# Sharing runs of eight edge records between blocks, and two pieces of work moved inside the edge loops of a two-layer graph kernel

## The reference, cut to what matters

```python
# layer 0: attention over edges, keyed by src
score = a_s[:, src] + a_d[:, dst] + aw_e[:, None] * elem[None, :] + ab[:, None]
w = jnp.exp(-jax.nn.relu(score / 20.0))
pooled = segment_sum(w * feats[:, dst], src); row_sum = segment_sum(w, src)
out = pooled / row_sum
# then a mixture of 16 experts, top 2
# layer 1: relations, keyed by dst
rel_e = rel_emb[etype]
alpha = exp(leaky_relu(h[src] @ w_src + h[dst] @ w_dst + rel_e @ w_rel))[:, None]
alpha = alpha / sum(alpha, axis=1, keepdims=True)      # one column: alpha is 1
agg = segment_sum((h[src] + rel_e) @ weight_neighbor * alpha, dst)
# then a dense feed-forward over the better half of the nodes
```

## Time and profile before

| | |
|---|---|
| time before, median of 3 runs | 2547.16 us (2541.32 to 2551.01) |
| the profiled execution | 2546.9 us, span 2545.2 us |
| busy over the span | PE 70%, DVE 77%, POOL 54%, ACT 14% |
| first stage (sort of layer 0, its table) | to 321 us |
| edge loop of layer 0 | 321 to 938 us |
| expert stage | about 1053 to 1467 us |
| edge loop of layer 1 | about 1585 to 2266 us |

### The profile page before, as it was taken

How to read it: one execution, slowest core, us unless ns; L and a number is a source line. 1 busy time by engine, 2 the same in 40 slices (tenths; PEclk the granted TensorE clock), 3 DMA queues, 4 the chain that set the end, 5 groups by cost and what they waited for, 6 DMA issues and landing times. The chain is left out here.

```text
span 2545.2 us, 41027 instructions
## 1 busy us (share of the span) xinstructions
PE 1787.7 (70%) x9989; PEld 1323.2 (52%) x9989; DVE 1962.6 (77%) x5413; ACT 367.8 (14%) x1302; POOL 1377.7 (54%) x1250
## 2 busy tenths in 40 slices
PE   0699357777777745499999934666666666567997
PEld 0698234445444424489998923333333333335776
DVE  8987898888888866587777356788888888776395
ACT  0000100000000002012221214011111111014331
POOL 0486077777777720148888500777777777610200
PEclk9999766676777655699999967677787786667999
DMA  2000144554545551589998841777767777941001
GB/s 91 2 4 12 52 119 133 133 131 133 132 132 133 126 54 52 184 283 293 295 298 279 277 143 59 214 203 201 198 195 199 196 199 196 155 61 35 27 0 50
DMA packets 204203, 361.38 MB, mean 142 GB/s; under 512 B 37152, under 2 KB 111580, under 8 KB 203996
## 3 DMA queue, kind: packets, MB, share of 16 engines
q0 software_dynamic: 64000, 175.79, 27.5%
q1 hardware_dynamic: 139196, 181.82, 23.1%
q10 hardware_dynamic: 928, 2.75, 0.3%
HBM read 334.42 MB, written 25.84 MB: 142 GB/s over the span
## 5 line engine op out<-in xcount | busy, mean ns | idle before, releaser
L960 POOL DMA_INDIRECT e_rows<-table,e_gidx x952 | 925.1, 972 | 322.5 <-issue 277.7
L1197 PE MATMUL e_psO<-e_rows,e_oh 128*128 128x260 f32 x928 | 382.2, 570 | 34.6 <-DVE acc L1025 29.4
L1025 DVE TENSOR_TENSOR acc<-acc,e_psO 128x260 f32 (+1 forms) x708 | 349.7, 494 | 47.3 <-PE e_psO L1197 12.9
L1925 PE MATMUL e_psO<-e_rows,e_oh 128*128 128x456 bf16 x488 | 232.4, 476 | 149.9 <-DVE e_oh L1887 149.8
L1197 PEld LDWEIGHTS e_psO<-e_rows,e_oh 128*128 128x128 f32 x928 | 233.7, 274 | 123.8 <-DVE acc L1025 68.6
L1098 PE MATMUL e_psA<-e_own_of_unit,e_ohT 128*128 (+2 forms) x952 | 115.0, 179 | 210.1 <-DVE e_sc L1154 111.9
L1098 PEld LDWEIGHTS e_psA<-e_own_of_unit,e_ohT 128*128 128x128 bf16 x952 | 86.3, 99 | 328.6 <-issue 318.8
L640 POOL DMA_INDIRECT records<-ordered,s_chunk x68 | 122.0, 1793 | 119.2 <-ACT ordered L625 103.3
L1927 PE MATMUL e_psO<-e_rows,e_oh 128*128 128x256 bf16 x488 | 172.5, 353 | 0.0
L1926 PE MATMUL e_psO<-e_rows,e_oh 128*128 128x256 bf16 x488 | 171.9, 352 | 0.0
L1491 POOL DMA_INDIRECT ln_xn<-token_rows,slot_row x64 | 99.3, 1552 | 126.2 <-POOLq L102 104.8
(11 more groups left out here) (367 smaller groups left out, 3655.1 us busy)
## 6 DMA issues: line engine op xcount, KB each, us to landing
hot_run<-in_L_ffn_w_dram SPq DMA_DIRECT2D x107, 512.0 KB, 6.2
XN<-in_L_ffn_w_dram SPq DMA_DIRECT2D x85, 512.0 KB, 5.0
e_edge_row<-edge_rows SPq DMA_DIRECT2D x122, 256.0 KB, 4.3
e_rows<-table,e_gidx POOLq DMA_INDIRECT x952, 3.0
e_edge_row<-edge_rows SPq DMA_DIRECT2D x116, 128.0 KB
table<-frow SPq DMA_DIRECT2D x25, 192.5 KB, 2.2
table<-frow SPq DMA_DIRECT2D x25, 130.0 KB, 1.9
token_rows<-ln_xn SPq DMA_DIRECT2D x25, 128.0 KB, 1.7
```

Source lines behind the costliest of these rows:

```text
L960: pool.indirect_dma_start(out=rows[:, r, t, 0:width], out_offset=None, in_=table, in_offset=bass.IndirectOffsetOnAxis(ap=gidx[:, r, t:t + ...
L1025: v.tensor_tensor(d, d, psO[:, units * (r % (4 // units)) + j, 0:accw], ALU.add).then_inc(S["added"], 1)
L1197: return pe.matmul(out[:, 0:A0], oh[:, r, t, :], rows[:, r, t, :], start=start, stop=stop)
L1925: pe.matmul(out[:, 0:A1], lhs, row[:, 2 + 2 * D:T1 + R], start=start, stop=False)
```

## The change

1. **Numbering through all blocks.** `starts` first sums the counts over the blocks of a bucket, so that a bucket's edges are numbered through all 17 blocks without padding between them. Where one block's run ends inside a chunk, the next block goes on in the same chunk. The scatters of both blocks name that chunk, so each scatter now adds (`compute_op=ALU.add`) to a list that was set to zero, and a block's scatters wait until the earlier block's scatters to the same list have landed. Layer 0 has two such lists for alternate blocks (`COPIES = (2, 1)`); both are loaded and one DVE addition (`merge`) joins them.
2. **Fewer units.** The formula loses the padding by blocks: 439 units in place of 463 in layer 0 (110 groups in place of 116), 232 in place of 244 in layer 1 (116 in place of 122). A block may now hold two partial chunks a bucket, so its matrices have 109 rows (ROWS) in place of 104; the scatters still name 112.
3. **Layer 1's marks and running counts in the loop of layer 0.** The 26 compares and 17 scans leave the first stage. DVE's loop in layer 0 does two compares in every four groups for 13 turns, then two scans in every four groups for 8 turns, and the last scan and the totals behind the loop.
4. **Relation marks on ACT.** In layer 1 ACT makes them: per group four `Abs` of (column - type), 200 columns each, and one `Relu` of 1 - that over 4 x 200, ahead by two groups.

```diff
-    ROWS = -(-(EP * CB + NT * (CK - 1)) // COLS)
+    ROWS = -(-(EP * CB + NT * 2 * (CK - 1)) // COLS)
-    UNITS = [(E + NBLK * NT * (CK - 1) + NT * (u * P - 1)) // (u * P) for u in TPUS]
+    UNITS = [(E + NT * (u * P - 1)) // (u * P) for u in TPUS]
+    COPIES = (2, 1)
...
         def scatter(self, pool, k, ordered):
             pool.wait_ge(self.kept, k + 1)
+            n = COPIES[self.l]
+            if k >= n:
+                pool.wait_ge(self.scattered[k % n], 16 * KC * (k // n))
             for j in range(KC):
                 pool.indirect_dma_start(
-                    out=rec_d[self.l], out_offset=...
-                    in_offset=None).then_inc(self.scattered, 16)
+                    out=rec_d[self.l][k % n], out_offset=...
+                    in_offset=None, compute_op=ALU.add).then_inc(self.scattered[k % n], 16)
...
+        def merge(self, dve, copies):
+            dve.wait_ge(self.landed, 16 * len(copies))
+            nc.vector.tensor_tensor(copies[0], copies[0], copies[1], ALU.add).then_inc(self.merged, 1)
...
                 dn.pipeline(sp, 0, 0, store)
-                es.load(sp, lines[:, :, :])
+                sp.wait_ge(es.put, NBLK)
+                es.load(sp, (lines[:, :, :], lines_b))
...
-                es1.buckets(link, keyi, keyb, raw[:, 1, :], raw[:, 0, :])
+                es1.buckets(link, keyi, keyb1, raw[:, 1, :])
+                es1.pack(link, keyi, raw[:, 1, :], raw[:, 0, :])
                 link(v.tensor_copy(es1.field[:, :, 1], raw[:, 2, :]))
-                link(es1.runs(link))
+                es.merge(dve, (lines[:, :, :], lines_b))
                 es.number_rows(dve, link, lines, rowi[:, :, :], rowb)
...
+            def l1_hot(q, r):
+                if r % 2 == 0:
+                    b = (q - 1) * 2 + r // 2
+                    nc.vector.tensor_scalar(es1.hot[:, :, bass.ds(b, 1), :]..., keyb1..., iota[0:EP, bass.ds(b, 1)],
+                                            None, ALU.is_equal).then_inc(bucket_marked, 1)
+            def l1_runs(q, r):
+                if r % 2 == 0:
+                    k = (q - (1 + HOT_TURNS)) * 2 + r // 2
+                    nc.vector.tensor_tensor_scan(flat_run[0:EP, at], flat_hot[0:EP, at], flat_hot[0:EP, at],
+                                                 0.0, ALU.add, ALU.max).then_inc(block_run, 1)
...
-            def l1_onehots(v, at, rows, S):
+            def l1_counts(act, at, rows, S):
                 g, q, r = at
                 counts = rows[:, r, :, :].bitcast(BF16)
+                act.wait_ge(S["counted"], g)
                 for t in range(TPG):
-                    ins = v.tensor_scalar(counts[:, t, T1:T1 + R], iota_b[:, :], etype1[...], None, ALU.is_equal)
-                ins.then_inc(S["counted"], 1)
+                    ins = nc.scalar.activation(away[:, t, :], iota_b[:, :], ACT.Abs, scale=-1.0, bias=etype1[...])
+                ins.then_inc(measured, 1)
+                back(act, S["summed"], g, DEPTH)
+                act.wait_ge(measured, g + 1)
+                nc.scalar.activation(counts[:, :, T1:T1 + R], away[:, :, :], ACT.Relu, scale=-1.0, bias=ones[:, 0:1])\
+                    .then_inc(S["counted"], 1)
```

More of the change, by code:

```diff
@@ L128, in ring, with pipeline @@
     def ring(G, depth):
-        def pipeline(eng, ahead, behind, step, beside=None, turns=0):
+        def pipeline(eng, ahead, behind, step, beside=None, turns=0, beside2=None, turns2=0):
             for s in range(-ahead, depth):
@@ L140, in pipeline @@
                         beside(q, r)
-            with eng.Fori(1 + turns, G // depth - 1) as q:
+            if beside2:
+                with eng.Fori(1 + turns, 1 + turns + turns2) as q:
+                    for r in range(depth):
+                        step(None, (q, r))
+                        beside2(q, r)
+            with eng.Fori(1 + turns + turns2, G // depth - 1) as q:
                 for r in range(depth):
@@ L433, in keep_moves, with buckets @@
             tag = f"s{self.l}_"
-            self.marked, self.put, self.kept, self.scattered, self.landed, self.turned = (
-                sem(tag + n) for n in ("marked", "put", "kept", "scattered", "landed", "turned"))
+            self.marked, self.put, self.kept, self.landed, self.merged, self.turned = (
+                sem(tag + n) for n in ("marked", "put", "kept", "landed", "merged", "turned"))
+            self.scattered = [sem(tag + f"scattered{i}") for i in range(COPIES[self.l])]
             self.rowed, self.row_stored = sem(tag + "rowed"), sem(tag + "row_stored")
-        def buckets(self, link, keyi, keyb, key, other):
+        def buckets(self, link, keyi, keyb, key):
             v = nc.vector
@@ L496, in starts @@
                                  run[:, 0:NBLK - 1, NB - 1:NB].to_broadcast([P, NBLK - 1, NB]), ALU.subtract))
+            link(v.scalar_tensor_tensor(by_block(flat[3]).rearrange("p k b -> p b k"), by_bucket(flat[6]), -float(CK),
+                                        ahead, ALU.mult, ALU.add))
             base = self.base[:, :, :]
[L499 to L504, removed]
+            level = base.rearrange("p k b -> p (k b)")
+            link(v.scalar_tensor_tensor(level, flat[2][0:EP, :], float(CK), earlier[0:EP, 0:nn], ALU.mult, ALU.add))
+            link(v.scalar_tensor_tensor(level, flat[3][0:EP, :], -1.0, level, ALU.add, ALU.add))
+            link(v.tensor_tensor(base[:, :, 1:], base[:, :, 1:], self.run[:, :, 0:NB - 1, CB - 1], ALU.subtract))
         def units(self, link, work):
@@ L1040, in step @@
                         post["payload"][0](dve, v, now, rows, psA, sc, oh, S)
-                    if nxt is not None and post.get("onehots"):
-                        post["onehots"](v, nxt, rows, S)
                     if now is not None and len(post["payload"]) > 1:
                         post["payload"][1](dve, v, now, rows, psA, sc, oh, S)
-                pipeline(dve, 2, 2, step)
+                pipeline(dve, 2, 2, step, post.get("dve_beside"), post.get("dve_turns", 0),
+                         post.get("dve_beside2"), post.get("dve_turns2", 0))
+                if post.get("dve_after"):
+                    post["dve_after"](dve)
             @block.scalar
@@ L1059, in step @@
                 def step(s, dyn):
-                    soon, now = (locate(s, dyn, d) for d in (3, 0))
+                    soon, nxt, now = (locate(s, dyn, d) for d in (3, 2, 0))
                     if now is not None:
@@ L1064, in step @@
                         indices(soon)
+                    if nxt is not None and post.get("counts"):
+                        post["counts"](act, nxt, rows, S)
                 pipeline(act, 3, 0, step, post.get("act_beside"), post.get("turns", 0))
```

114 lines of the change are left out of this document (81 added, 33 removed).

## The result

The changed kernel takes 2482.26 us (2480.22 to 2485.93, four runs) where the kernel before took 2546.7 beside it: 0.975 of the time, 95% interval 0.9727 to 0.9772. That is 64 us less; 111 were forecast, so the time is inside the range of 2408 to 2505 and 46 us above the number. The profiled execution has a span of 2479.4 us.

What follows compares the result with a forecast made beforehand. Serial stages, each with its own limit: PE in the first and expert stages, POOL in layer 0's loop, DVE and POOL in layer 1's. Terms -22.3 - 37.9 + 10.6 + 1 + 2.6 - 43 - 24 + 2 = -111 gave 2436 us, range 2408 to 2505.

Steps and rivals of the forecast that it cites:

- The empty tiles' price: Ends of both edge loops: 1.81 and 1.79 us per empty tile; fewer of them save 37.9 and 43 us.
- The compares and scans at the first stage's end: First stage: moving layer 1's compares, scans and totals out lets DVE end 28.3 us sooner (30.5 to 26).
- The longer `starts` and `units`: Front of the first stage: 9.8 us before, 13.6 after, so +3.8.
- covered, as argued: First stage: adding scatters cost nothing, as 33 us lie between the last scatter and the list's load.
- The last scan with the totals: Behind layer 0's loop: 1.4 + 1.1 us, so +2.6.
- `place`: First stage on PE: loading 109 columns for 104 costs +2.2 us (0, or +7 if all of it grew).
- The scans: Layer 0's loop: 16 scans stretch POOL's gathers by 0.66 us each, +10.6 (0 to +22.6).
- Layer 1's pace: Layer 1's loop: 5.07 us a group with relation marks off DVE, -24 us; the rival that it stays, 12%.
- I take nothing there too: Expert stage: adding scatters cost nothing, as POOL waits 30.0 us for ACT there and PE is the limit.
- 68x - 30: Expert stage's growth in us if each of its 68 adding scatters costs x us more.
- the longer `starts`: Expert stage: falls on DVE, which PE waits for at times, +2 us (0 to 3.8).
- adding scatters cost POOL more: Rival: x us more each delays first stage and expert stage; 2491 us at x = 0.94. Mild 18%, slower 6%.

Runs made afterwards that it cites:

- the spread rows: Kernel after, empty edge slots gathering rows spread over the table, run together with two other repairs: empty tiles 16.7 and 33.5 us, whole 2417.24 us.
- Repair (b): Kernel after, scans in layer 0's loop taking their second input from PSUM, run with two other repairs: 428 gathers 547.45 us, whole 2417.24 us.
- Repair (a): Kernel after, expert stage's marks taking their second input from PSUM, run with two other repairs: stage 407.8 us, whole 2417.24 us.
- adding alone: Kernel before with layer 1's scatters adding and its relation counts on ACT, old numbering and 104 columns: 2553.15 us, 1.0019; expert stage 435.0 us.
- the first runs: Plain scatters in layer 1, 112 columns, counts back on DVE (kernel after), groups cut alone (kernel before), where the kernel before takes 2800.68 us: 0.9642 to 0.9688.
- the kernel with 112 columns: Kernel after with 112 columns in place of 109, three more than the numbering needs: 2711.21 us, 0.9685 of the kernel before.

## Why the prediction was half right

**Right.** The direction, and the mechanism of most terms. The empty tiles' price (22.3 and 42.9 us measured, 22.8 and 43 forecast) and its cause, shown by the spread rows. The compares and scans at the first stage's end, 28.3 us, shown by putting them back (28.7). The longer `starts` and `units`, 13.9 us in place of 13.6. In the first stage the adding scatters take 2253 ns on average (1793 before) and still end at 271 us, ahead of the list's load at 292: covered, as argued (their time was forecast to stay near 1.8). The last scan with the totals, 2.6 us. No table load stands in layer 1's loop, as the Trainium skill's page ScalarE: Activation LUTs, section Table sets: the hidden batching unit, says of cheap functions; this trace shows it for `Abs` and `Relu`. They take 450 and 962 ns each, where I had 364 and 840; ACT is still busy only 59% of that loop (236.8 of 400 us).

**Mis-sized.** `place`: I took 2.2 us from two weight loads of different stages and kept "+7 if all of it grew" as the far end; the truth is 8.4, a little past that far end. That alone is the first stage's miss. The scans: 0.66 us each were taken from the average stretch of the scatters; the 128 gathers of their groups took 175.3 us, 13.4 more than the 128 before them, 0.84 for each of the 16, between that and the full 1.4. Repair (b) gave back 13.3. The whole loop's 428 gathers took 17.9 us more, forecast 11.6. For one gather beside a scan the bound by the Trainium skill's page SBUF — State Buffer, section Who interferes with whom, was nearer at times: the one at 661.16 beside the scan at 661.09 took 2.18 us, its own 0.95 and most of the scan's 1.50. The same section says that a DVE instruction with at most one SBUF input, outside the two-port modes, doesn't contend; repairs (a) and (b) agree, with token DMAs of 3.2 to 4.7 us beside the marks falling to 1.78 at most, and gathers of up to 2.19 us beside the scans to 1.07. Layer 1's pace: 5.17 us for 5.07, as gathers there still take 0.988 us on average, four with their gaps 5.15; I had taken a value between no stretch and the 0.98 of before.

**The step that failed** is "I take nothing there too", and the price beside it, 68x - 30. The cost x itself was small, about 0.5 us by the shortest scatters; the 68 scatters of the stage together rose by 27.2 us, from 84.0 to 111.2. But POOL's 30.0 us of waiting for ACT were no reserve: only 6.5 of them were filled, and 23.5 us of waiting stand there still, again in 12 times (22.2 us in 12 with adding alone). The waits stand in a cycle of three steps in which POOL gathers tokens, writes results back and scatters, and PE had already waited 10.7 us for token rows. My reading is that a wait behind which POOL immediately has to catch up can't be filled with other work; no run tests that by itself. What I should have summed is POOL's cycle: six token DMAs, two of them stretched to 3 to 4 us by the marks, and four scatters, with ten gaps, against the 18.8 us of three steps. In the cycle read above that sum was 18.1 before and is 20.3 after. Repair (a) shows that it takes both: with the stretching gone and the scatters still adding, PE no longer waits for token rows (over 0.15 us at a time), and the stage is shorter than before the change.

How the 29.9 us are made up: 2.2 come only from where the stage is counted. In this trace the first token row landed 2.2 us sooner behind the first gather than before (5.1 us, not 7.3) and the second no sooner (8.5 us in both), so the count starts 2.2 us sooner; from the second row on it grew by 27.7. The gates date those. Against the kernel before they are 6.8 us late at the sixth, behind PE's wait of 4.9 us for DVE's product above; 3.6 late at the 11th to the 17th, with the first scatter behind the 12th; and 27.6 late at the last. So the longer `starts`, which I gave 2 (0 to 3.8), leave 3.6 us, and 24.0 come while the scatters run. By the sixth gate the kernels with the new `starts` whole are 6.0 to 6.9 us late (six of them), those with the old ones not at all (three of them). With adding alone the gates are 0.5 us early up to the 14th and 21.1 late at the last, so 21.6 of the 24.0 is adding. What the other 2.4 are isn't shown; `mark`'s largest compare, 2.99 us for 2.86, is as much over 17 blocks. On the chip of the first runs adding is worth only 7, so its price belongs to the chip as well as to the kernel.

By its own form the rival "adding scatters cost POOL more" (mild, 18%) came true in the expert stage alone, at a higher price than its formula gives for x = 0.5 (4 us). That the time lies in the range is in part luck: the upper end was drawn for x = 0.94 with a first stage 21 us late, and what filled the room was 28 us in the expert stage at half that x, with 6, 6 and 11 us from three mis-sized terms, all to the slow side.

## What to carry to other kernels

Slack of an engine that is off the critical path is counted over its own cycle, gaps and stretched instructions included; a sum of its waits over a stage is no reserve. Before work is moved beside POOL's indirect DMAs, look at what DVE does at that time: moving one of two SBUF inputs to PSUM gave back 34 us in one stage (from the second token row on) and 13 in another, at a copy of 0.25 us a block on DVE in the first. Padding that is read has a price by where it reads: spread its addresses.

## What the runs showed of the hardware

An indirect DMA that adds takes POOL 1.45 us at the shortest for 112 rows of 64 bytes, where one that only writes takes 0.94, with 0.30 us between two of either.

The chips differ by more than the change is worth. On one of the two with 2800 us DVE stood in layer 0's loop for 42 us in 200 without a wait that the profile can name, up to 2.9 us at a time; in the kernel after, the same stretch lists no such wait of DVE. Two of the lines, of DVE's waits in the kernel with 112 columns, 500 to 700 us:

```profile
DVE acc L1081 <- issue: 25.2, 19, 2.9
DVE e_sc L1213 <- issue: 7.0, 5, 1.8
```

There the groups of both loops take 6.2 to 6.3 us in place of 5.0 to 5.2, and scans and counts hardly move that: the 440 gathers of layer 1 take 683.7 to 685.3 us with the counts on ACT and 685.9 to 688.2 with them on DVE. The cause wasn't tried.
